# Row maxima of attention scores: one VectorE instruction for two heads, over two neighbouring PSUM banks

## The chip, the core and the metric

One NeuronCore of a Trainium2 chip runs the whole kernel. The metric is the device time of one execution in microseconds (us). The engines are TensorE (PE: matmuls and transposes; PEld: its weight loads), VectorE (DVE), ScalarE (ACT), GpSimd (POOL) and SyncE (SP, which here only issues DMAs). Each engine runs its own instructions in order; they meet only at semaphores.

## What is computed

A gated cross-attention block and a quantised gated feed-forward, each with a residual. B is 8 items of S = 256 rows and E = 256 columns; 16 heads of width 16. Cut to what matters:

```python
def xattn(Q, ctx):                      # Q = layernorm(x)
    q, k, v = heads(Q @ Wq.T), heads(ctx @ Wk.T), heads(ctx @ Wv.T)   # (8, 16, 256, 16)
    attn = where(mask, q @ k.T / sqrt(16), -inf)                      # (8, 16, 256, 256)
    return merge(softmax(attn, axis=-1) @ v) @ Wo.T + bo

x = x + tanh(g_xattn) * xattn(layernorm(x), ctx)
x = x + tanh(g_ffn) * ffn(layernorm(x))     # ffn: 8-bit fake quantisation, silu(gate) * up, down
```

All masks are true in the inputs used, so that the branch without masks runs.

## The kernel before, in words

**Parts of the program.** (1) Projections of the eight items to q, k, v. q and k are split into three bf16 parts, stored to DRAM and loaded back as stacks (`q_st`, `k_st`). The projections of items 6 and 7 are mixed with the first scores of item 0. (2) The attention, one step for each item b. (3) The feed-forward. The change touches the end of (1) and all of (2).

**The softmax in two passes.** The exponentials need the maximum of each score row beforehand. So the scores are computed twice. For the maxima, `scores_for_max` (L1408; `early_scores`, L1314, for item 0) computes 256 x 256 scores of one head with rows on partitions: two matmuls for the two row halves c = 0, 1, side by side in one PSUM bank of 512 f32 columns. `maxima` (L910) takes the negated maximum of both halves with one `tensor_reduce` into `neg_max[:, p, c, h]`. TensorE transposes the maxima of eight heads at a time (`max_tr`, L1298), ScalarE copies them to SBUF (`max_copy`, L724), GpSimd splits them into two bf16 parts (`max_split`, L544 and L545), and a DMA from SyncE's queue puts them as extra rows under `q_st` (`max_rows`, L419). Then `scores_for_exp` (L1422) computes the transposed scores less the maximum, ScalarE takes the exponential (`exp`, L763), and `product_with_v` (L1439) multiplies by v.

**One step** (b, the same order on each engine, written out in the code). On TensorE, for h = 0 to 15: scores for the exponential of head h of item b; then the scores for the maxima of head h+2 of item b+1 (for h = 14 and 15: heads 0 and 1 of item b+2); then what the table `PE_AT` puts at this h: at h = 1 the `max_tr` of heads 8 to 15 of item b and the second half of the product with v of item b-1 (`("pv", 1)`), at h = 3 `project_out` of row half 1 (L1448), at h = 9 the `max_tr` of heads 0 to 7 of item b+1 and `("pv", 0)`, at h = 11 `project_out` of row half 0. On VectorE, for h = 0 to 15: what `DVE_AT` puts at h, then `maxima` of head h of item b+1. `DVE_AT` gives: h = 3 `back` (L1033), h = 4 `turn` (L1009, waits for the product with v), h = 5 the reciprocals (`rec`, L1015), h = 9 `back` (waits for GpSimd's `scale_heads`, L578), h = 12 `row_max` (L1060, from step 3 on), two `stats` (L1047, from step 2 on) and `turn`, h = 13 `rec` and `means` (L1055).

**PSUM banks.** The scores for the maxima go to `bank_b`, four banks, head h in bank h % 4. TensorE may write head h only when the maximum of head h-4 has been taken: `pe.wait_ge(max_done, H * b + h - 3)`, and `maxima` waits for `a_done`, one count for each head. The scores for the exponential rotate over three banks of `bank_a` and wait for ScalarE's `exp`.

**GpSimd in one step:** `max_split` of heads 8 to 15 of item b (it gates the exponential scores of heads 8 and later, over the DMA), `add_bias`, `v_copy`, `residual` (L570), `scale_heads` (L578; gates `back`), `max_split` of heads 0 to 7 of item b+1, `residual` (waits for ScalarE's `scaled_out`, L772), `scale_heads`, and for item b-2 `second_rstd` (L493 to L500) and `hat` (L561).

**The end of the projections.** `project_and_maxima` (L989) on VectorE takes, for each of items 6 and 7, two maxima, a `residue` (L995), two maxima, a `residue`, and four more maxima. TensorE interleaves `early_scores` with the projection's matmuls.

Of the kernel before, what the change touches and what calls it, by code (L numbers as in the profile page):

```python
# [21 lines left out]
P = 128  # L22
ALU = mybir.AluOpType
ACT = mybir.ActivationFunctionType
AX = mybir.AxisListType
# [40 lines left out]
def flamingo_block(nc, x, ctx_in, mask_rows, mask_full, g_xattn, g_ffn, Wq, Wk, Wv, Wo, bo,  # L66
# [3 lines left out]
    H = 16  # L70
    D = E // H
    EC = E // P
    QC = S // P
# [12 lines left out]
    HH = H // 2  # L86
# [40 lines left out]
    with ExitStack() as stack:  # L127
        def sb(name, shape, dt=F32):
            return stack.enter_context(nc.sbuf_tensor(name, shape, dt))

        def pb(name, shape, dt=F32):
            return stack.enter_context(nc.psum_tensor(name, shape, dt))

        def sem(name):
            return stack.enter_context(nc.semaphore(name))
# [14 lines left out]
        ident_f = sb("ident_f", [P, P])  # L150
# [2 lines left out]
        tg_bo = sb("tg_bo", [P, E])  # L153
        wd_scale = sb("wd_scale", [P, E])
        wd_diag = sb("wd_diag", [P, EC, P])
        neg_max = sb("neg_max", [P, 2, QC, H])
        max_f = sb("max_f", [HH, 2, S])
        max_parts = sb("max_parts", [HH, 2, 2, S], BF16)
        rec = sb("rec", [P, 2, NB])
# [70 lines left out]
        bank_b = pb("bank_b", [P, 4, 512])  # L230
# [33 lines left out]
        a_done, max_done = sem("a_done"), sem("max_done")  # L264
# [71 lines left out]
        def at_head(places, h, b, p, known=B, ahead=True):  # L336

            return [(what, b - at // H if at >= H else b, (p, 1 - p)[at // H % 2]) for what, at in places.items()
                    if at % H == h and at // H <= known and (ahead or "next" not in what)]
# [537 lines left out]
        def _(dve):  # L877
# [29 lines left out]
                dve.wait_ge(ct_done, b + 1)  # L907
                dve.tensor_copy(ctx_t[:, p], bank_b[:, 2 + p]).then_inc(ctx_t_ready, 1)

            def maxima(b, p, h, bank):  # L910
                dve.wait_ge(a_done, H * b + h + 1)
                dve.tensor_reduce(neg_max[:, p, :, h], bank.rearrange("p (c s) -> p c s", c=QC),  # L912
                                  axis=AX.X, op=ALU.max, negate=True).then_inc(max_done, 1)

            def residue(b, p, w):
                dve.wait_ge(hi_done, 2 * b + w + 1)
# [72 lines left out]
            def project_and_maxima(b, p, first):  # L989

                for w in range(2):
                    maxima(0, 0, first + 2 * w, bank_b[:, 2 * w])
                    maxima(0, 0, first + 2 * w + 1, bank_b[:, 2 * w + 1])
                    dve.wait_ge(hi_done, 2 * b + w + 1)
                    dve.tensor_tensor(resid[:, p, w], bank_a[:, w], parts[:, p, w, HI[w]], ALU.subtract  # L995
                                      ).then_inc(res_done, 1)
                for h in range(first + 4, first + HH):
                    maxima(0, 0, h, bank_b[:, h % 4])

            project_and_maxima(6, 0, 0)  # L1000
            project_and_maxima(7, 1, HH)


# [90 lines left out]
            def other(what, b, p):  # L1094
                if what[0] == "row_max":
                    row_maxima(b)
                elif what[0] == "means":
                    row_means(b, p)
                elif what[0] == "stats":
                    row_stats(b, what[1])  # L1100
                elif what[0] == "turn":
                    turn(b, what[1])
                elif what[0] == "rec":
                    reciprocals(b, what[1])
                else:
                    back(b, p, what[1])

            def step(b, p, known=B):


                for h in range(H):
                    for what, of, q in at_head(DVE_AT, h, b, p, known):
                        other(what, of, q)
                    maxima(b + 1, 1 - p, h, bank_b[:, h % 4])

            def groups(b, pair, g=slice(0, 2), turns=1):

# [33 lines left out]
            for b in range(B - 1):  # L1151
                step(b, b % 2, b)
# [110 lines left out]
        def _(pe):  # L1263
            mm, tr = nc.tensor.matmul, nc.tensor.transpose
# [28 lines left out]
            def max_tr(b, p, half, to, used):  # L1293
                if used:
                    pe.wait_ge(*used)
                pe.wait_ge(max_done, H * b + HH * (half + 1))
                for c in range(QC):
                    done = tr(to[0:HH, c * P:(c + 1) * P], neg_max[:, p, c, HH * half:HH * (half + 1)], ident_f[:])  # L1298
                done.then_inc(mt_done, 1)

            def early_scores(h, masked):
# [62 lines left out]
            def project_and_scores(b, p, j, first, masked):  # L1364

                def scores(n):
                    early_scores(first + n, masked)
                    if first and n == 1:
                        max_tr(0, 0, 0, bank_m, (w_ready, 4))

                project(b, p, j, ahead=False, between=scores)
                for n in range(6, HH):
                    scores(n)
# [27 lines left out]
            def attend(masked):  # L1401
# [50 lines left out]
                def other(what, b, p, of, q, known):  # L1452

                    if what == "max_tr":
                        max_tr(b, p, 1, ring_bank(b, what), ring_free(b, what, known))
                    elif what == "next_max_tr":
                        max_tr(b + 1, 1 - p, 0, ring_bank(b, what), ring_free(b, what, known))
                    elif what[0] == "out":
                        project_out(of, q, min(what[1], 1), ring_bank(b, what), ring_free(b, what, known))
                    else:  # L1460
                        for g in range(2 * what[1], 2 * what[1] + 2):
                            product_with_v(of, q, g, known == 0 and g == 0)
# [179 lines left out]
```

## Time and profile before

| | us |
|---|---|
| median of 3 executions | 254.37 (254.21 to 257.52) |
| the profiled execution, own time | 256.14 |
| its span, first to last instruction | 254.6 |
| VectorE busy | 212.6 (84%) |
| TensorE busy | 212.0 (83%) |
| ScalarE busy | 160.1 (63%) |
| GpSimd busy | 138.0 (54%) |
| mean granted TensorE clock | 0.960 |

The profile is of one execution. Its own time stands 1.5 us above its span, and it is 1.8 us (0.7%) above the median of the three; the durations below are the profile's. A busy share is an average over stages with different limits, so that it names no bound by itself.

### The profile page before, as it was taken

What the parts mean: (1) busy time and instruction counts of PE and PEld (TensorE: products, weight loads), DVE (VectorE), ACT (ScalarE), POOL (GpSimd) and SP (SyncE); (2) the same over time, 40 slices, a digit from 0 to 9 for tenths busy, and PEclk for the clock granted to TensorE, in tenths of its full rate; (3) what the DMA queues carried; (4) which work ended last, traced back from release to release, by engine and by line L of the source; (5) the groups of instructions that cost most, each with busy time, mean ns of one, the idle gap of its engine ahead of it and who ended that gap; (6) DMA issues with size and microseconds to landing.
All of it is one profiled execution on the core that took longest, in us unless ns stands there. A gap on an engine that the chain in (4) does not pass through costs nothing.

```text
span 254.6 us, 5343 instructions
## 1 busy us (share of the span) xinstructions
PE 212.0 (83%) x1661; PEld 145.1 (57%) x1664; DVE 212.6 (84%) x419; ACT 160.1 (63%) x293; POOL 138.0 (54%) x241
## 2 busy tenths in 40 slices
PE   0899799979989999999999999989592898853970
PEld 0688688857746666666666666645361443312850
DVE  3378699979898998988989898969957779998992
ACT  2347476476687766667677666677726588865920
POOL 7446467643452536285675838389835433330590
PEclk9999999999999999999999999999979599996897
DMA  6999948999546653455436152000000600000296
GB/s 219 236 295 295 299 134 226 272 258 259 145 140 167 130 124 97 102 127 125 128 98 139 45 138 83 4 0 4 1 0 0 206 3 1 0 4 0 25 144 167
DMA packets 34185, 30.80 MB, mean 121 GB/s; under 512 B 5232, under 2 KB 27760, under 8 KB 34160
## 3 DMA queue, kind: packets, MB, share of 16 engines
q1 hardware_dynamic: 29776, 27.74, 40.2%
q0 software_dynamic: 1360, 1.31, 4.2%
q10 hardware_dynamic: 3024, 1.44, 2.1%
q8 instruction: 13, 0.21, 0.4%
q14 instruction: 12, 0.10, 0.1%
HBM read 20.65 MB, written 9.70 MB: 119 GB/s over the span
## 4 chain that ended last, share of the span: by engine, by line
PE 35%; DVE 27%; issue 10%; ACT 9%; POOL 7%; DMA 5%; SPq 4%; ACTq 0%; POOLq 0%; DVEq 0%
PE bank_o L1439 9%; PE bank_a L1422 6%; PE bank_b L1408 4%; PE bank_a L1448 3%; ACT arena L763 3%; DVE h_max L1200 3%; PE bank_a L1325 3%; DMA big<-in_ctx 3%; DVE big L1209 2%; DMA big<-max_parts 2%; DVE arena L1237 2%; DVE arena L902 2%; DVE v_all L1243 2%; POOL big L486 1%; DVE resid L917 1%
## 5 line engine op out<-in xcount | busy, mean ns | idle before, releaser
L912 DVE TENSOR_REDUCE neg_max<-bank_b 128x2 f32<-128x512 f32 x128 | 80.1, 672 | 4.9 <-PE bank_b L1314 3.0
L1422 PE MATMUL bank_a<-big 98*128 98x256 bf16 x256 | 48.8, 274 | 6.2 <-ACT arena L763 2.3
L763 ACT ACTIVATE arena<-bank_a 128x512 f32<-128x512 f32 x64 | 34.3, 605 | 13.9 <-PE bank_a L1422 13.8
L1408 PE MATMUL bank_b<-big 96*128 96x256 bf16 x224 | 42.7, 272 | 0.3 <-issue 0.2
L763 ACT ACTIVATE big<-bank_a 128x512 f32<-128x512 f32 x64 | 33.9, 595 | 12.4 <-PE bank_a L1422 12.1
L1422 PEld LDWEIGHTS bank_a<-big 98*128 98x128 bf16 x256 | 20.2, 97 | 25.4 <-issue 8.8
L1325 PE MATMUL bank_a<-arena,w_t 128*128 128x256 f32 x128 | 30.8, 387 | 0.2 <-issue 0.2
L1325 PEld LDWEIGHTS bank_a<-arena,w_t 128*128 128x128 f32 x128 | 23.6, 194 | 3.6 <-issue 0.6
L510 POOL TENSOR_TENSOR arena<-resid,arena 128x512 bf16<-128x512 f32 x16 | 18.3, 1160 | 10.7 <-ACT arena L701 10.7
L1408 PEld LDWEIGHTS bank_b<-big 96*128 96x128 bf16 x224 | 21.1, 97 | 4.5 <-issue 0.8
L570 POOL TENSOR_TENSOR x_rows<-x_rows,arena 128x256 f32<-128x256 f32 x14 | 11.6, 833 | 15.4 <-ACT arena L772 15.4
L850 ACT ACTIVATE arena<-bank_b,w_scale_x 128x512 f32<-128x512 f32 (+1 forms) x24 | 16.1, 685 | 6.0 <-PE bank_b L1574 2.0
L650 POOL TENSOR_TENSOR big<-arena 128x512 f32<-128x512 f32 x8 | 10.1, 1267 | 17.3 <-ACT arena L854 17.3
L1574 PE MATMUL bank_b<-arena,wgu_t 128*128 128x512 bf16 (+1 forms) x57 | 16.2, 394 | 3.1 <-DVE big L1209 2.9
L544 POOL CAST max_parts<-max_f 8x256 bf16<-8x256 f32 x16 | 6.4, 399 | 21.9 <-issue 19.4
L692 ACT ACTIVATE arena<-bank_a 128x512 bf16<-128x512 f32 x16 | 9.4, 595 | 13.3 <-PE bank_a L1325 8.2
L1009 DVE STREAM_TRANSPOSE arena<-bank_o 128x512 f32<-128x512 f32 (+1 forms) x17 | 11.5, 679 | 7.3 <-PE bank_o L1439 7.3
L1439 PE MATMUL bank_o<-arena,v_cur 128*32 128x256 f32 x256 | 15.7, 382 | 1.3 <-DVE arena L1009 1.3
L1336 PE MATMUL bank_o<-w_t,arena 128*128 128x256 f32 x64 | 15.6, 381 | 0.0
L1439 PE MATMUL bank_o<-big,v_cur 128*32 128x256 f32 x256 | 15.5, 382 | 0.0
L1200 DVE TENSOR_REDUCE h_max<-big 128x1 f32<-128x512 f32 (+1 forms) x24 | 15.1, 668 | 0.0
L1448 PE MATMUL bank_a<-w_t,arena 128*128 128x256 f32 x56 | 14.5, 381 | 0.1
(179 smaller groups left out, 437.7 us busy)
## 6 DMA issues: line engine op xcount, KB each, us to landing
qk_parts<-arena SPq DMA_DIRECT2D x8, 768.0 KB, 5.5
big<-qk_parts SPq DMA_DIRECT2D x32, 192.0 KB, 3.3
big<-qk_parts SPq DMA_DIRECT2D x32, 128.0 KB, 3.3
x_rows<-in_x SPq DMA_DIRECT2D x8, 256.0 KB, 6.3
big<-qk_parts SPq DMA_DIRECT2D x32, 64.0 KB, 3.5
big<-in_ctx SPq DMA_DIRECT2D x7, 256.0 KB, 4.9
out<-x_rows SPq DMA_DIRECT2D x7, 256.0 KB, 2.8
out<-v_all POOLq DMA_DIRECT2D x5, 256.0 KB, 6.3
```

Source lines behind the costliest of these rows:

```text
L510: pool.tensor_tensor(parts[:, p, w, LO[w]], resid[:, p, w], parts[:, p, w, MID[w]], ALU.subtract).then_inc(lo_done, 1)
L763: act.activation(probabilities(h), ring_bank(b, ("exp", h)).rearrange("p (c s) -> p c s", c=QC), ACT.Exp, scale=SCALE).then_inc(exp_done, 1)
L850: act.activation(silu[0:r, c % 3], bank_b[0:r, c % 3], ACT.Silu, scale=w_scale_x[0:r, c:c + 1]).then_inc(silu_done, 1)
L912: dve.tensor_reduce(neg_max[:, p, :, h], bank.rearrange("p (c s) -> p c s", c=QC), axis=AX.X, op=ALU.max, negate=True).then_inc(max_done, 1)
L1200: chain.then(dve.tensor_reduce(h_max[0:r, tile(u)], h_all[0:r, c, bass.ds(n * CW, CW)], axis=AX.X, op=ALU.max, apply_absolute_value=True))
L1325: last = mm(bank_a[:, w, f * S:(f + 1) * S], w_t[:, w, k, f * P:(f + 1) * P], src[:, p, k * S:(k + 1) * S], start=(k == 0), stop=(k == EC ...
L1336: last = mm(bank_o[:, c * E:(c + 1) * E], ctx_t[:, p, k * S + c * P:k * S + (c + 1) * P], w_t[:, 2, k], start=(k == 0), stop=(k == EC - 1))
L1408: done = mm(to, q_st[0:KR, p, h, c * P:(c + 1) * P], k_st[0:KR, p, h], start=True, stop=not masked)
L1422: done = mm(to, k_st[0:KM, p, h, k * P:(k + 1) * P], q_st[0:KM, p, h], start=True, stop=not masked)
L1439: done = mm(bank_o[n * 2 * D:(n + 1) * 2 * D, g % 2 * S:(g % 2 + 1) * S], v_cur[:, p, k, h], probabilities(h)[:, k], start=(k == 0), stop= ...
L1448: done = mm(to[:, 0:E], att_t[:, p, f, c * P:(c + 1) * P], w_t[:, 3, f], start=(f == 0), stop=(f == EC - 1))
L1574: last = mm(to, wgu_t[:, g, k, c * P:c * P + r], xq_t[:, k, bass.ds(n * CW, CW)], start=(k == 0), stop=(k == EC - 1))
```

## The change

`neg_max` is laid out with the row halves innermost. `maxima` now takes heads h and h+1 (h even) in one `tensor_reduce` that reads banks h % 4 and h % 4 + 1 (four rows of 256 columns for each partition) and writes four neighbouring values; it waits until the scores of both heads are there and raises `max_done` by 2 at its end. In the steps it is issued at odd h, behind what `DVE_AT` puts there; at even h only the items of the table are issued. TensorE's order and all its waits stay as they are. The transposes of the maxima read `neg_max` with a stride of 2 in place of 1.

```diff
-        neg_max = sb("neg_max", [P, 2, QC, H])
+        neg_max = sb("neg_max", [P, 2, H, QC])
...
-            def maxima(b, p, h, bank):
-                dve.wait_ge(a_done, H * b + h + 1)
-                dve.tensor_reduce(neg_max[:, p, :, h], bank.rearrange("p (c s) -> p c s", c=QC),
-                                  axis=AX.X, op=ALU.max, negate=True).then_inc(max_done, 1)
+            def maxima(b, p, h):
+                banks = bank_b[:, h % 4:h % 4 + 2]
+                dve.wait_ge(a_done, H * b + h + 2)
+                dve.tensor_reduce(neg_max[:, p, h:h + 2], banks.rearrange("p h (c s) -> p h c s", c=QC),
+                                  axis=AX.X, op=ALU.max, negate=True).then_inc(max_done, 2)
...
             def project_and_maxima(b, p, first):
                 for w in range(2):
-                    maxima(0, 0, first + 2 * w, bank_b[:, 2 * w])
-                    maxima(0, 0, first + 2 * w + 1, bank_b[:, 2 * w + 1])
+                    maxima(0, 0, first + 2 * w)
...
-                for h in range(first + 4, first + HH):
-                    maxima(0, 0, h, bank_b[:, h % 4])
+                for h in range(first + 4, first + HH, 2):
+                    maxima(0, 0, h)
...
                     for what, of, q in at_head(DVE_AT, h, b, p, known):
                         other(what, of, q)
-                    maxima(b + 1, 1 - p, h, bank_b[:, h % 4])
+                    if h % 2:
+                        maxima(b + 1, 1 - p, h - 1)
...
-                    done = tr(to[0:HH, c * P:(c + 1) * P], neg_max[:, p, c, HH * half:HH * (half + 1)], ident_f[:])
+                    done = tr(to[0:HH, c * P:(c + 1) * P], neg_max[:, p, HH * half:HH * (half + 1), c], ident_f[:])
```

## Rows read from the trace of the kernel before

**Rows 1.** Part 1 of the page: busy us, share of the span, instructions.
```profile
PE 212.0 (83%) x1661; PEld 145.1 (57%) x1664; DVE 212.6 (84%) x419; ACT 160.1 (63%) x293; POOL 138.0 (54%) x241
```

**Rows 2.** Part 4 of the page: the chain that ended last, by engine, by line.
```profile
PE bank_o L1439 9%; PE bank_a L1422 6%; PE bank_b L1408 4%; PE bank_a L1448 3%; ACT arena L763 3%; DVE h_max L1200 3%; PE bank_a L1325 3%; DMA big<-in_ctx 3%; DVE big L1209 2%; DMA big<-max_parts 2%; DVE arena L1237 2%; DVE arena L902 2%; DVE v_all L1243 2%; POOL big L486 1%; DVE resid L917 1%
```

**Rows 3.** The instructions of line L912, and who waited for them (us, times).
```profile
L912 DVE TENSOR_REDUCE neg_max<-bank_b x128: 627/680/694, 56.0 to 166.5; 128x2 f32<-128x512 f32 x128
...
  PEld bank_b L1408: 0.7, 3
```

**Rows 4.** Two other VectorE reductions, by line and form: count, busy us, mean ns.
```profile
L935 DVE TENSOR_REDUCE mask_sum<-mask_u 128x4 f32<-128x1024 uint8 x4 | 4.8, 1207 | 0.0
...
L983 DVE TENSOR_REDUCE w_amax<-wd_rows 128x2 f32<-128x1408 f32 x1 | 1.6, 1605 | 0.0
```

**Rows 5.** Timeline of VectorE, steps 3 and 7: start us, us, instruction, count.
```profile
117.14 0.45 DVE L1033 STREAM_TRANSPOSE arena<-arena 128x256 f32<-128x256 f32 x1 [0.48 <-POOL arena L578]
117.51 1.85 DVE L912 TENSOR_REDUCE neg_max<-bank_b 128x2 f32<-128x512 f32 x3
119.28 0.67 DVE L1060 TENSOR_REDUCE row_max<-v_all 128x2 f32<-128x512 f32 x1
119.87 0.74 DVE L1047 BATCH_NORM_STATS2 stats<-x_rows 128x6 f32<-128x256 f32 x2
120.53 0.70 DVE L1009 STREAM_TRANSPOSE arena<-bank_o 128x512 f32<-128x512 f32 x1
121.15 0.66 DVE L912 TENSOR_REDUCE neg_max<-bank_b 128x2 f32<-128x512 f32 x1
...
121.98 3.65 DVE L912 TENSOR_REDUCE neg_max<-bank_b 128x2 f32<-128x512 f32 x6
...
180.08 0.70 DVE L1009 STREAM_TRANSPOSE arena<-bank_o 128x512 f32<-128x512 f32 x1
180.81 0.25 DVE L1017 RECIPROCAL rec<-arena 128x16 f32<-128x16 f32 x1
```

**Rows 6.** Timeline of TensorE, from head 8 of step 3 to head 8 of step 4.
```profile
116.62 0.39 PE L1422 MATMUL bank_a<-big 98*128 98x256 bf16 x2 [0.16 <-DMA big<-max_parts]
...
122.32 0.38 PE L1422 MATMUL bank_a<-big 98*128 98x256 bf16 x2
122.54 0.38 PE L1408 MATMUL bank_b<-big 96*128 96x256 bf16 x2
...
123.63 0.39 PE L1422 MATMUL bank_a<-big 98*128 98x256 bf16 x2 [0.27 <-ACT arena L763]
...
124.88 1.93 PE L1439 MATMUL bank_o<-arena,v_cur 128*32 128x256 f32 x32
...
131.06 0.39 PE L1422 MATMUL bank_a<-big 98*128 98x256 bf16 x2 [0.24 <-DMA big<-max_parts]
```

**Rows 7.** Timeline of VectorE where step 0 begins.
```profile
68.62 9.06 DVE L912 TENSOR_REDUCE neg_max<-bank_b 128x2 f32<-128x512 f32 x15 [0.29 <-PE bank_b L1314]
```

**Rows 8.** Timeline of TensorE where step 0 begins, to the first transpose of maxima.
```profile
69.21 0.60 PE L1408 MATMUL bank_b<-big 96*128 96x256 bf16 x4 [0.19 <-issue]
...
69.97 0.39 PE L1408 MATMUL bank_b<-big 96*128 96x256 bf16 x2
70.20 0.38 PE L1422 MATMUL bank_a<-big 98*128 98x256 bf16 x2
...
70.80 0.38 PE L1298 MATMUL bank_a<-ident_f,neg_max 128*8 128x128 f32 x2
```

**Rows 9.** The chain in order of time at the same place: start us, us, what.
```profile
70.40 1.06 ACT big L763 x2
71.46 0.25 ACT max_f L724
...
73.81 1.77 DMA big<-max_parts
75.63 0.39 PE bank_a L1422 x2
```

## The prediction

> **What bounds the kernel now.** I read the busy times first. VectorE and TensorE are both at five sixths of the span [rows 1], and L912, the line that changes, is the costliest of all: 128 instructions of about 0.68 us [rows 3]. A reader who stops there expects most of what is saved at L912 to be gained.
>
> The chain of waits says otherwise. Among its largest parts are the matmuls L1439, L1422 and L1408, ScalarE's exponential and the DMA of the maxima; of the feed-forward's VectorE work some stands there too; L912 does not [rows 2]. The question from the other side, who waited for L912, gives 0.7 us in all, in three waits [rows 3]. That is all that a shorter L912 alone could give back on TensorE's side. So VectorE is almost full in the attention and yet bounds it hardly anywhere.
>
> One step shows why. It is 14.44 us long (head 8 of step 3 at 116.62, of step 4 at 131.06) [rows 6]. VectorE's cost of an instruction is the distance between starts, since consecutive records overlap: 15 maxima in 9.06 us, each record 0.68 long, make (9.06 - 0.68) / 14 = 0.60 us each [rows 3, 7]. In the same way row_max costs 0.59, the two stats 0.66, a turn 0.62, back 0.37, rec and means together 0.23 (121.98 less the end of the maximum at 121.15 + 0.60) [rows 5]. A step is 16 x 0.60 for the maxima and 0.59 + 0.66 + 2 x 0.62 + 2 x 0.37 + 0.23 + 0.15 (the second rec, an estimate from the first) = 3.6 for the rest, 13.2 us of 14.44. VectorE has 1.2 us to spare in each step and spends part of it waiting for GpSimd before back [rows 5]. Head 8 of each step waits for the DMA that brings the maxima, by 0.24 us in step 4 [rows 6]; that DMA is GpSimd's, and GpSimd's work before it hangs on the previous step's project_out, not on VectorE.
>
> **The change, part by part.**
>
> *The instruction.* No row shows an f32 reduction over two PSUM banks. The nearest are reductions of one row set of 1024 columns, 1.207 us, and of 1408, 1.605 us, 1.04 ns for each further column [rows 4]. Against 0.68 us for 512 columns the second 512 cost 0.53, so that a pair should show a record of about 1.21 us and cost 0.60 + 0.53 = 1.13 us, where two cost 1.20. Saved: 0.07 for each of 64 pairs, 4.3 us of VectorE's time, 0.5 us in a step. Bounds: below, nothing but the columns is paid, 2 x 0.53 = 1.06; above, the two records end to end, 2 x 0.68 = 1.36. I take 1.13, because the 1024-column row is the nearest. By rows 2 and 3 the saving lies beside other work; I book it at 0, at most -0.7 (all that TensorE waited for L912).
>
> The trace thus shows 0.07 us as what an instruction costs beside its columns. The Trainium skill (VectorE: DVE Perf Modes, Side-by-side: where the cycles go for N=2048 bf16) gives some 150 cycles of init and decode for each instruction, and its Rules for kernel authors say to minimise the count of operations. By that, 64 removed instructions would be about 10 us less VectorE work, an estimate from the page; rows 7 say 4.3 at most, because the start of an instruction overlaps the end of the one before.
>
> *The release of banks.* This is the loss. TensorE may write head h when the maximum of head h-4 is taken. Before, an even head was free 0.68 us after its own start; now it is free with the odd one, after 1.21 us, and the instruction cannot start before the odd head's scores are there. Four banks become two pairs.
>
> *Start of step 0.* TensorE's first score matmuls of item 1 run right behind VectorE: the ones at 69.97 come 0.07 after the end of the second record of the run at 68.62 (68.62 + 0.60 + 0.68 = 69.90) [rows 7, 8]. After the change: heads 12 and 13 of item 0 from 68.62 (the run still waits for head 13's scores) to 69.83, heads 14 and 15 from 69.75 to 70.96. Head 0 of item 1 needs head 12: 69.90 instead of 69.21. Head 2 needs head 14, so the second pair: 71.03 instead of 69.97. The exponential scores of head 1 stand behind it in TensorE's queue: 71.25 instead of 70.20; then head 3 and the transpose of the maxima, at 71.7 instead of 70.80. ScalarE copies the maxima behind the exponential of head 1, that is at 72.2 instead of 71.46, and from there the chain runs through GpSimd and the DMA to head 8 at 75.63 [rows 9]. So +0.7 us, on the chain of waits, and what follows (products with v, exponentials) moves with it. Bounds: 0.4 (the second pair ends only 0.45 later than the third of three single maxima, if the order behind it lets the rest be caught up) and 1.0.
>
> In the interleaved part before, each residue (L995) comes about 0.5 later, since its pair ends later than the second single maximum did. ScalarE reads it behind other copies, and only from 69.0 on is it busy without a gap; I book 0, at most +0.2.
>
> *A step with all the extra work (from step 3 on).* Back at 117.14 waits for GpSimd [rows 5]; before, the maximum of head 8 was taken during that wait, now heads 8 and 9 come behind back. From its end at 117.51: two pairs 2.26, row_max 0.59, stats 0.66, turn and rec 0.62 + 0.23, and a wait of rec for turn. That wait was hidden by a maximum between them; rows 5 show it bare in step 7, 180.08 to 180.81, 0.73 against 0.62, so 0.1. Heads 12 and 13 start at 121.97, are done at 123.18. TensorE wants bank 0 for head 0 of the item after next at 122.54, at h = 14 [rows 6]: it stalls until 123.25, 0.7 us. Behind it wait the exponential scores of head 15, then ScalarE. Heads 14 and 15 are done 1.13 later, at 124.31; head 2 is written at 124.38, the exponential scores of head 1 at 124.60, the transpose 125.04, and the product with v at 125.35 instead of 124.88: +0.47. Until head 8, ScalarE's four exponentials are late by that, and head 8 waits for the DMA anyway (0.24) and for the exponential of head 5; there some 0.2 to 0.3 is left. That delay reaches GpSimd through project_out and comes back to back one step later, so that it counts once in two steps. Steps 3, 4 and 5 have the stall (step 6 issues no scores ahead at h = 14): 0.1 each, +0.3. Bounds: 0 (all hidden by the DMA wait) and 3 x 0.47 = +1.4.
>
> Rec now runs right behind turn, ahead of the next maxima, so GpSimd's scale_heads and second_rstd are not made late by it. The waits that the change adds hold no other engine's DMA. The strided read in the transposes concerns 32 weight loads of 8 columns; 0.
>
> *Sum.* 0 + 0.7 + 0 + 0.3 = +1.0 us. For the profiled execution 256.14 + 1.0 = 257.1, span 255.6. The profiled execution stood 0.7% above the median, so for the median 254.37 + 1.0 = 255.4.
>
> **The rivals.**
>
> *A: VectorE's time counts.* If the chain is only apparent, and every step is in truth paced by VectorE's 13.2 us with its waits, all of 4.3 us comes back: 250.1. For it: 84% busy. Against it: 0.7 us of waits for L912, and a wait for TensorE or GpSimd in each step. It decides where a step's idle time on VectorE is gone; a partial form gives 252.
>
> *B: two banks in one read cost more than 1.13.* At 1.36 a step is 8 x 1.36 + 3.7 = 14.6 us, above 14.44: VectorE becomes the bound, 0.15 in each of 6 steps, and the stalls above grow by 3 x 0.23 = 0.7 each, of which steps 3 to 5 pass on most. With 0.7 + 0.3 at the start that is 0.9 + 1.0 + 2.1 = 4.0, so 258.4. The point from which it decides is (14.44 - 3.7) / 8 = 1.34 us for a pair.
>
> *C: the stall at h = 14 is passed on whole.* Where the TensorE-ScalarE loop itself is the bound, nothing hides it: +0.7 at the start and 1.4 to 2.1 in steps 3 to 5, 256.5 to 257.2, taken as 256.8.
>
> *D: nothing is seen.* The start is caught up during step 0, where VectorE is ahead, and the rest is hidden: 254.4.
>
> The Trainium skill (Advanced Engine Details and Errata, TRN2 Errata) lists reading several PSUM banks with one instruction among its workarounds; that speaks against B, and no row here shows such a read.
>
> **How the numbers follow.** The forecast (+0.5 to +1.5) has 0.40, C 0.18, D 0.20, A 0.10 (a third of it below 251), B 0.12. The predicted time is 255.4. The range goes down to the partial form of A, 252.3, and up beyond B's 258.4 to 258.6. 2% is 5.1 us, about what a measurement of this kernel can tell from no change: faster than 249.3 needs more than all of A, 0.03; slower than 259.5 needs a pair beyond 1.36 us, half of B, 0.06; within, 0.91.
>
> **What would show each step right or wrong.** L912 should be 64 records of 1.2 us with 128x4 outputs; VectorE's busy time lower by some 3 us, TensorE's the same, its idle time up. In step 0 head 8 should start near 76.3. L1408 should wait for L912 well beyond 0.7 us, mostly once a step at h = 14 from step 3 on. Rec should follow turn at once. The forecast is wrong if the span falls by over 2 us (then A), if a pair's record is 1.3 us or more (B), or if head 8 of step 0 stays at 75.6 (D).

## The result and the profile after

The changed kernel takes 1.0086 times the time before, 95% interval 1.0054 to 1.0118, over 20 executions of each. Both figures leave out the executions that took over 1.5% longer than the fastest of their kernel, 5 before and 3 after. On the median that the prediction started from, 254.37 us, that is 256.6 us: +2.2 us where +1.0 was forecast, outside the forecast's own band of +0.5 to +1.5 and within 2%. The profiled execution shows 257.1 us of span against 254.6.

The instruction is what was expected, and it did not help. Line L912 is now L913 (lines behind it move by one or stay). Part 5 of the page and, below it, who waited for L913 (us, times), the rows that answer to [rows 3] and [rows 4]:

```profile
L913 DVE TENSOR_REDUCE neg_max<-bank_b 128x4 f32<-128x1024 f32 x64 | 75.5, 1210 | 9.6 <-PE bank_b L1315 4.9
```

```profile
  PE bank_b L1315: 4.9, 6
  PE bank_b L1409: 4.2, 8
...
  PEld bank_b L1409: 3.5, 8
  PE bank_b L1409: 2.5, 6
  PE bank_b L1315: 0.2, 1
```

The first two lines of the second fence are VectorE waiting for scores before L913; the last three are TensorE and its weight loads waiting for L913. Those were 0.7 us in three waits before [rows 3]; they are 3.5 us in 8 waits and 2.5 us in 6 now (the two overlap: the matmul at 125.25 below waits 0.59 us and its weight load 0.87, for the same record of L913), and 0.2 us in one wait of the early scores, L1315. And L913 has entered the chain that ended last, where L912 was absent [rows 2]; part 4 of the page, by line:

```profile
PE bank_o L1440 8%; PE bank_a L1423 6%; PE bank_b L1409 6%; DVE neg_max L913 4%; DMA big<-in_ctx 3%; DVE h_max L1201 3%; PE bank_a L1449 3%; PE bank_a L1326 2%; DVE big L1210 2%; DVE arena L1238 2%; DVE arena L902 2%; DVE v_all L1244 2%; DVE stats L1047 1%; DVE arena L1009 1%; ACT arena L763 1%
```

**Where the time went.** Two executions drift apart by a few tenths of a microsecond before the changed part begins (the first early score matmul starts at 55.60 before, 55.91 after). Measured from that matmul, the attention repeats within 0.01 us from run to run where its waits are the same, as layout_only below shows, so I use the stretch that begins there as a ruler. Its end is the product with v at h = 1 of step 7, the last in the chain ahead of the closing VectorE work, which starts at 168.26 before and 170.83 after: 112.66 and 114.92 us from the ruler's start, +2.26. (The product with v behind it, at h = 9 of step 7, is 2.11 later than before.) From there to the end of the span both take 86.3 us, so that in these two executions the whole loss lies in the changed part. Three stretches of each, up to the ruler, the ruler, and behind it (from:to, us; busy us and instructions of PE, PEld, DVE, ACT and POOL; granted TensorE clock, DMA share, GB/s):

```profile
0.00:55.60 55.60, 45.11 (x231) 38.69 (x232) 41.10 (x96) 28.60 (x52) 32.53 (x75) 1.00 0.88 248
55.60:168.26 112.66, 106.64 (x1024) 71.79 (x1028) 102.08 (x196) 79.44 (x164) 62.18 (x112) 1.00 0.47 120
168.26:254.60 86.34, 60.23 (x410) 34.58 (x413) 69.47 (x128) 52.09 (x79) 43.28 (x56) 0.88 0.20 41
```

```profile
0.00:55.91 55.91, 46.22 (x231) 39.64 (x232) 40.73 (x96) 28.84 (x52) 32.81 (x75) 1.00 0.89 248
55.91:170.83 114.92, 107.41 (x1025) 71.42 (x1027) 100.31 (x132) 80.00 (x164) 62.04 (x112) 1.00 0.45 117
170.83:257.10 86.27, 60.94 (x414) 34.62 (x413) 69.57 (x128) 52.10 (x80) 42.91 (x56) 0.86 0.20 41
```

The granted clock is 1.00 (2.4 GHz) over the ruler in all ten profiles, so that it has no part in what the ruler shows. Behind the ruler it is 0.86 to 0.89 and the stretch takes 83.7 to 86.3 us, with the same code in every run: that the two kernels agree there to 0.1 us is chance, and spans of single executions can't show an effect of 2 us.

Timelines of TensorE in the changed kernel, the places where the time goes:

```profile
55.91 0.38 PE L1315 MATMUL bank_b<-big 96*128 96x256 bf16 x2
...
63.20 0.38 PE L1315 MATMUL bank_b<-big 96*128 96x256 bf16 x2 [0.18 <-DVE neg_max L913]
...
70.71 0.60 PE L1409 MATMUL bank_b<-big 96*128 96x256 bf16 x4 [1.04 <-DVE neg_max L913]
...
71.76 0.39 PE L1409 MATMUL bank_b<-big 96*128 96x256 bf16 x2 [0.23 <-DVE neg_max L913]
71.98 0.38 PE L1423 MATMUL bank_a<-big 98*128 98x256 bf16 x2
...
72.43 0.38 PE L1299 MATMUL bank_a<-ident_f,neg_max 128*8 128x128 f32 x2
...
77.18 0.39 PE L1423 MATMUL bank_a<-big 98*128 98x256 bf16 x2 [1.08 <-DMA big<-max_parts]
```

From the ruler's start, head 0 of item 1 comes at 14.80 (before 13.61, [rows 8]), the transpose of the maxima at 16.52 (before 15.20), head 8 of step 0 at 21.27 (before 20.03): +1.24. Before that stands a stall that the prediction had not seen, at 63.20: head 8 of item 0 waits for the pair of heads 4 and 5. The same matmul started at 62.55 before, 6.95 from the start; now 7.29, +0.34. VectorE's row that answers to [rows 7]:

```profile
69.34 8.08 DVE L913 TENSOR_REDUCE neg_max<-bank_b 128x4 f32<-128x1024 f32 x7 [0.35 <-PE bank_b L1315]
```

It begins 13.43 us from the ruler's start, 0.41 later than before (68.62 - 55.60 = 13.02). Its first pair, heads 12 and 13, ends at 69.34 + 1.22 = 70.56, and head 0 of item 1 follows at 70.71 in the fence above. The chain that ended last goes through the second pair, heads 14 and 15, into head 2 of item 1 at 71.76 and on to ScalarE, the rows that answer to [rows 9]:

```profile
70.48 1.23 DVE neg_max L913
...
71.76 0.39 PE bank_b L1409 x2
72.15 0.23 PE bank_a L1423 x2
...
72.41 0.60 ACT big L763
73.00 0.26 ACT max_f L724
```

In step 3, TensorE and VectorE of the changed kernel:

```profile
124.28 0.38 PE L1423 MATMUL bank_a<-big 98*128 98x256 bf16 x2
125.25 0.39 PE L1409 MATMUL bank_b<-big 96*128 96x256 bf16 x2 [0.59 <-DVE neg_max L913]
```

```profile
119.10 0.45 DVE L1033 STREAM_TRANSPOSE arena<-arena 128x256 f32<-128x256 f32 x1 [0.63 <-POOL arena L578]
119.47 2.32 DVE L913 TENSOR_REDUCE neg_max<-bank_b 128x4 f32<-128x1024 f32 x2
121.70 0.67 DVE L1060 TENSOR_REDUCE row_max<-v_all 128x2 f32<-128x512 f32 x1
122.29 0.74 DVE L1047 BATCH_NORM_STATS2 stats<-x_rows 128x6 f32<-128x256 f32 x2
122.95 0.70 DVE L1009 STREAM_TRANSPOSE arena<-bank_o 128x512 f32<-128x512 f32 x1
123.68 0.25 DVE L1015 RECIPROCAL rec<-arena 128x16 f32<-128x16 f32 x1
123.85 0.23 DVE L1055 BATCH_NORM_AGGREGATE mv_now<-stats 128x2 f32<-128x6 f32 x2
124.00 3.45 DVE L913 TENSOR_REDUCE neg_max<-bank_b 128x4 f32<-128x1024 f32 x3
```

The reader is to compare the two fences: head 0 of the item after next stands behind 124.28 in TensorE's queue and wants its bank at 124.50; the pair of heads 12 and 13 starts at 124.00 and ends at 125.21; the matmul starts at 125.25. Between back (119.10, which waited for GpSimd) and that pair now stand the maxima of four heads, row_max, stats, turn, rec and means; between back and the maximum of head 12 there stood three maxima, row_max, stats and turn before [rows 5].

### The profile page after: what moved, and what is told of

The parts are those of the page before. It is cut to its first block, busy times and chain, and to the rows that moved or that the text cites. A ratio compares the mean times of both kernels' runs of the same rounds, so it can differ in the third digit from the quotient of the medians.

```text
span 257.1 us, 5346 instructions
## 1 busy us (share of the span) xinstructions
PE 214.6 (83%) x1664; PEld 145.7 (57%) x1664; DVE 210.6 (82%) x355; ACT 160.9 (63%) x293; POOL 137.8 (54%) x241
## 4 chain that ended last, share of the span: by engine, by line
PE 35%; DVE 33%; issue 11%; ACT 7%; POOL 5%; DMA 4%; SPq 3%; ACTq 0%; DVEq 0%; POOLq 0%
PE bank_o L1440 8%; PE bank_a L1423 6%; PE bank_b L1409 6%; DVE neg_max L913 4%; DMA big<-in_ctx 3%; DVE h_max L1201 3%; PE bank_a L1449 3%; PE bank_a L1326 2%; DVE big L1210 2%; DVE arena L1238 2%; DVE arena L902 2%; DVE v_all L1244 2%; DVE stats L1047 1%; DVE arena L1009 1%; ACT arena L763 1%
## 5 line engine op out<-in xcount | busy, mean ns | idle before, releaser
L913 DVE TENSOR_REDUCE neg_max<-bank_b 128x4 f32<-128x1024 f32 x64 | 75.5, 1210 | 9.6 <-PE bank_b L1315 4.9
L1326 PE MATMUL bank_a<-arena,w_t 128*128 128x256 f32 x128 | 32.1, 399 | 0.5 <-issue 0.5
L1326 PEld LDWEIGHTS bank_a<-arena,w_t 128*128 128x128 f32 x128 | 24.5, 201 | 4.3 <-issue 0.9
L1409 PEld LDWEIGHTS bank_b<-big 96*128 96x128 bf16 x224 | 20.3, 97 | 9.3 <-DVE neg_max L913 3.5
L1575 PE MATMUL bank_b<-arena,wgu_t 128*128 128x512 bf16 (+1 forms) x60 | 17.1, 398 | 2.6 <-DVE big L1210 2.6
```

The costliest lines, as they stand in the source:

```text
L913: dve.tensor_reduce(neg_max[:, p, h:h + 2], banks.rearrange("p h (c s) -> p h c s", c=QC), axis=AX.X, op=ALU.max, negate=True).then_inc(ma ...
L1326: last = mm(bank_a[:, w, f * S:(f + 1) * S], w_t[:, w, k, f * P:(f + 1) * P], src[:, p, k * S:(k + 1) * S], start=(k == 0), stop=(k == EC ...
L1409: done = mm(to, q_st[0:KR, p, h, c * P:(c + 1) * P], k_st[0:KR, p, h], start=True, stop=not masked)
L1575: last = mm(to, wgu_t[:, g, k, c * P:c * P + r], xq_t[:, k, bass.ds(n * CW, CW)], start=(k == 0), stop=(k == EC - 1))
```

## Experiments

The ruler of each run (same two marks in its own chain and timeline), beside the ratio to the kernel before:

| run | ruler, us | against before | ratio (95% interval) |
|---|---|---|---|
| before | 112.66 | | |
| after | 114.92 | +2.26 | 1.0086 (1.0054 to 1.0118) |
| layout_only | 112.66 | 0.00 | 0.9967 (0.9926 to 1.0008) |
| pairs_start_only | 113.89 | +1.23 | 1.0042 (1.0005 to 1.0080) |
| pairs_steps_only | 113.69 | +1.03 | 1.0025 (0.9988 to 1.0062) |
| pairs_back_later | 114.49 | +1.83 | 1.0063 (1.0023 to 1.0103) |
| pairs_steps_back_later | 113.18 | +0.52 | 1.0007 (0.9968 to 1.0046) |
| pairs_but_last_four | 112.94 | +0.28 | 0.9988 (0.9951 to 1.0026) |
| single_half_columns | 112.66 | 0.00 | 1.0000 (0.9963 to 1.0037) |
| pairs_half_columns | 112.74 | +0.08 | 0.9992 (0.9944 to 1.0039) |

The intervals of the ratios are some 0.4% to each side, 1 us, so that most of these runs can't be told from each other by their times. The ruler resolves them, from one profiled execution each. The times confirm it where they can: the intervals of after, pairs_start_only and pairs_back_later lie above 1, and those of the others include it.

**layout_only**

`maximum` is the reduction of one head in the new layout; it stands in project_and_maxima too.

```diff
+            def maximum(b, p, h):
+                dve.wait_ge(a_done, H * b + h + 1)
+                dve.tensor_reduce(neg_max[:, p, h], bank_b[:, h % 4].rearrange("p (c s) -> p c s", c=QC),
+                                  axis=AX.X, op=ALU.max, negate=True).then_inc(max_done, 1)
...
-                    if h % 2:
-                        maxima(b + 1, 1 - p, h - 1)
+                    maximum(b + 1, 1 - p, h)
```

> The changed layout of neg_max and the transposes that read it with a stride of 2, but one instruction for each head as before, so this leaves only the layout of the change. Theory (the loss comes from the later release of banks): no difference, ratio 1.000 within 0.002, L912's instructions at 0.68 us, the waits for them under 1 us as before. Rival (the strided weight loads or the denser writes cost): part of the 1.0086, that is 1.003 to 1.009, with transposes of the maxima above 0.27 us.

Measured: ruler +0.00, ratio 0.9967. The layout, the denser writes and the strided transposes cost nothing. The transposes of the maxima have the same 272 ns and the wait for L912 the same 0.7 us as before.

**pairs_start_only and pairs_steps_only**

pairs_start_only has the last three lines of the edit above, on the changed kernel. pairs_steps_only leaves the steps of the changed kernel and has:

```diff
-                    maxima(0, 0, first + 2 * w)
+                    maximum(0, 0, first + 2 * w)
+                    maximum(0, 0, first + 2 * w + 1)
...
-                for h in range(first + 4, first + HH, 2):
-                    maxima(0, 0, h)
+                for h in range(first + 4, first + HH):
+                    maximum(0, 0, h)
```

> Pairs in the maxima of item 0 (project_and_maxima) alone, single maxima in all steps. Theory: TensorE waits for the pairs of heads 4, 5 and 12 to 15 of item 0; head 8 of step 0 starts 1.0 us later against the start of the projections of item 6, and nothing makes this good later: +1.1 us, ratio 1.004. Rival (the start is caught up in step 0, all loss is in the steps): ratio 1.000.

> Single maxima for item 0, pairs in all steps. Theory: step 0 begins as before; 0.4 us are lost in steps 0 and 1 at heads 0, 8 and 10 of the next item, and 0.6 us in steps 3 to 5 at h = 14 (a wait of 0.6 us for L912 in step 3): +1.0 us, ratio 1.004. Rival (the steps give back the saved VectorE time once the start does not hide it): ratio below 1.000, down to 0.985 if all 0.5 us of each step counts.

Measured: +1.23 and +1.03, together 2.26, exactly what the whole change costs. Eight of the 64 pairs make over half of the loss. In pairs_start_only the head 8 of step 0 is 1.23 late and stays 1.23 late in every product with v to the end: nothing is caught up, and nothing is added. In pairs_steps_only step 0's head 8 comes at 20.03 from the ruler's start, as before; the product with v at h = 1 of step 2 comes at 41.24, where it came at 40.83, so 0.41 late; the other 0.62 come in steps 3 to 5. So the rival, that the steps give back VectorE's saved time, is out.

**pairs_back_later and pairs_steps_back_later**

```diff
-              ("rec", 1): H + 5, ("back", 1): H + 9,
+              ("rec", 1): H + 5, ("back", 1): H + 10,
```

> The changed kernel with back of the second pair of groups moved from h = 9 to h = 10 in VectorE's order, so that the maxima of heads 8 and 9 are taken while GpSimd's scale_heads is awaited, as the maximum of head 8 was before. Theory: heads 12 and 13 are done 0.6 to 1.1 us earlier in steps 3 to 5, the wait of TensorE at h = 14 falls from 0.6 us to under 0.1, and 0.6 us come back: +1.6 us against the kernel before, ratio 1.006. Rival (the steps are held by the TensorE-ScalarE loop or GpSimd alone and the stall is hidden): ratio unchanged at 1.0086.

> Single maxima for item 0, pairs in the steps, back moved from h = 9 to h = 10. Theory: the losses add, so of 1.0 us for the pairs in the steps the 0.4 us are given back that the move gave back beside pairs at the start: last product with v 0.6 us later than before against the first scores of item 0, ratio 1.0024. Rival (the two are not independent): 1.0 us, or 0.

Measured: +1.83 and +0.52, so that the move of one instruction in VectorE's order gives back 0.43 and 0.51 of the 0.62 us of steps 3 to 5. VectorE of pairs_back_later at the same place:

```profile
117.37 2.50 DVE L913 TENSOR_REDUCE neg_max<-bank_b 128x4 f32<-128x1024 f32 x2 [0.52 <-PE bank_b L1409]
119.79 0.43 DVE L1033 STREAM_TRANSPOSE arena<-arena 128x256 f32<-128x256 f32 x1
120.14 1.19 DVE L913 TENSOR_REDUCE neg_max<-bank_b 128x4 f32<-128x1024 f32 x1
121.25 0.67 DVE L1060 TENSOR_REDUCE row_max<-v_all 128x2 f32<-128x512 f32 x1
```

Two pairs now stand ahead of back, which no longer waits for GpSimd, and row_max starts at 121.25 where it started at 121.70. TensorE's matmuls in this run have no wait for L913 left in step 3, and the weight load ahead of the second one 0.27 us (0.87 in the changed kernel):

```profile
124.42 0.38 PE L1423 MATMUL bank_a<-big 98*128 98x256 bf16 x2
124.80 0.39 PE L1409 MATMUL bank_b<-big 96*128 96x256 bf16 x2
```

The matmul comes 0.38 behind its neighbour instead of 0.97, so the wait in the records is gone, though not the last 0.16 us over the usual 0.22. Of the 0.19 and 0.11 us that are left of the 0.62, 0.12 and 0.11 come in one place: at h = 14 of step 5 the matmul still waits for L913, by 0.21 us, and the product with v behind it is that much later.

**pairs_but_last_four** (on pairs_steps_only)

```diff
+                    if h >= 12:
+                        maximum(b + 1, 1 - p, h)
-                    if h % 2:
+                    elif h % 2:
                         maxima(b + 1, 1 - p, h - 1)
```

> Single maxima for item 0; in the steps pairs for heads 0 to 11 and single maxima for heads 12 to 15, in the order of the kernel before; back at h = 9. 42 pairs are left of 64, so 2.8 us of VectorE time are saved as against 4.3. Theory: head 12 is done before TensorE wants its bank at h = 14, so the 0.6 us in steps 3 to 5 and 0.15 us in step 0 go; 0.25 us stay, for the pairs of heads 4 to 7 in step 1; ratio 1.001. Rival (every pair costs a little, wherever it is): two thirds of the 1.0 us of the steps, ratio 1.003.

Measured: +0.28. 42 pairs cost 0.28 us, of which 0.24 come in step 1, as expected; the 14 of heads 12 to 15 cost 0.75. What pairs cost depends on where they stand, and not on their number.

**single_half_columns and pairs_half_columns**

The first edit is on the kernel before, the second on the changed one.

```diff
-                  bank.rearrange("p (c s) -> p c s", c=QC),
+                  bank.rearrange("p (c s) -> p c s", c=QC)[:, :, 0:S // 2],
```

```diff
-                  banks.rearrange("p h (c s) -> p h c s", c=QC),
+                  banks.rearrange("p h (c s) -> p h c s", c=QC)[:, :, :, 0:S // 2],
```

> The kernel before, but each maximum is taken over the first 128 of the 256 columns of a row half; the other columns are left out, all else is the same work. L912 should fall from 0.68 to 0.41 us, 34 us of VectorE time in all. Theory (VectorE's time in the attention does not bound): the whole kernel gains 0 to 1.5 us, ratio 0.994 to 1.000. Rival (the 84% busy VectorE paces the steps): over 10 us faster, ratio under 0.96.

> The changed kernel, but each maximum is taken over the first 128 of the 256 columns of a row half; the other columns are left out. A pair's record should then be 0.68 us, as long as that of one head before. Theory (what costs is how long a pair holds two banks, not that two heads are tied together): TensorE no longer waits for L912 beyond what it did before, the loss of 2.2 us is gone, time within 0.5 us of the single maxima over half the columns, ratio 0.994 to 1.002. Rival (waiting for the odd head's scores is itself the cost): still over 1 us slower than the single maxima over half the columns.

Measured: 0.00 and +0.08. The record of one head fell to 0.411 us, as expected, and VectorE's busy time by 28 us, not by 34, since consecutive records overlap. The page and the instructions of L912 in single_half_columns:

```profile
PE 211.8 (83%) x1661; PEld 145.6 (57%) x1664; DVE 184.4 (73%) x419; ACT 160.1 (63%) x293; POOL 138.1 (54%) x241
```

```profile
L912 DVE TENSOR_REDUCE neg_max<-bank_b x128: 360/425/427, 56.4 to 166.5; 128x2 f32<-128x256 f32 x128
its engine sat idle before it (us, times) until:
  PE bank_b L1408: 13.2, 20
  PE bank_b L1314: 6.0, 9
```

VectorE is busy 28 us less than in [rows 1], and the ruler does not move by 0.01 us: the time is now idle time before L912 (19.2 us against 4.6), before turn (13.8 against 4.8) and before back (5.1 against 1.9). That is the clearest answer to rival A. It also shows that the 0.7 us of waits for L912 [rows 3] were worth nothing: they are 0.2 us here. In pairs_half_columns the instructions and the waits for them:

```profile
L913 DVE TENSOR_REDUCE neg_max<-bank_b x64: 652/692/693, 57.2 to 166.2; 128x4 f32<-128x512 f32 x64
...
who waited for it (us, times):
  PE bank_b L1409: 0.5, 1
```

A pair that holds its two banks for 0.69 us instead of 1.21 costs 0.08 instead of 2.26 us, although it still waits for the odd head's scores and takes the same place in VectorE's order. So the coupling of two heads by itself is worth 0.08 us at this length; the rest is the time for which the pairs hold their banks and stand in front of each other in VectorE's queue. The run shortens both together and does not part them.

## Why the prediction came out as it did

- **The bound.** Right. VectorE at 84% of the span bounded nothing in the attention: taking away 28 us of its work changed nothing there. Its busy time fell by 2.0 us with the change, 212.6 to 210.6, where some 3 was forecast. Rival A is refuted. The two rows that said so beforehand were the absence of L912 in the chain and the 0.7 us of waits for it.
- **The instruction.** Right. The record was forecast at 1.21 us and is 1.210; the distance between starts was forecast at 1.13 and is (8.08 - 1.22) / 6 = 1.14 in a run of seven from 69.34 and 1.12 in the run of three above. Rival B is refuted: a read over two neighbouring PSUM banks costs what its columns cost, 1.210 us beside the 1.207 us of 1024 columns in [rows 4]. The Trainium skill (Advanced Engine Details and Errata, TRN2 Errata) lists reading several PSUM banks with one instruction among its workarounds, and the trace agrees that it can be done.
- **The start of step 0.** The mechanism was right, the term was mis-sized: +0.7 forecast, with bounds of 0.4 and 1.0, and +1.23 measured by pairs_start_only. The working from head 12 of item 0 on holds once it starts later. What failed is the sentence on the interleaved part: it looked for who reads the residues and booked 0, and did not follow TensorE's own wait for the banks there. Head 8 of item 0 waits for the pair of heads 4 and 5, 0.34 us, and everything behind it moves; the run of pairs begins 0.41 later, and with the forecast's 0.7 that is 1.1 of the 1.23. The last 0.1 was lost in the forecast's own working: it has the exponential scores of head 1 at 71.25; the exponential follows 0.43 later and the copy of the maxima 0.59 behind that (71.98, 72.41 and 73.00 in the rows above), so the copy belonged at 72.27, +0.8, and not at 72.2, +0.7.
- **Steps 0 to 2.** Missed. The prediction costed only steps with the work of h = 12; 0.41 us are lost in steps 0 and 1, where the scores of heads 0, 2, 8 and 10 of the item ahead come 0.1 to 0.3 us later than usual, behind their pairs. VectorE had more to spare there, but a pair of banks comes back later all the same.
- **Steps 3 to 5.** The mechanism was right, and so were the place and about the size of the stall: 0.7 us forecast at h = 14 of step 3, 0.59 in the record of the wait. The product with v behind it was forecast 0.47 late and is 0.60 later than the ones ahead of it; at h = 9 of step 4 0.30 of that is left, where 0.2 to 0.3 was forecast. What was low is the share that is passed on: I took 0.1 a step from the argument that the delay counts once in two steps, and the steps cost 0.30, 0.16 and 0.16, in all 0.62 instead of 0.3.
- **The sum.** +1.0 forecast, about +2.2 measured: 0.5 too little at the start, 0.4 missed in steps 0 and 1, 0.3 too little in steps 3 to 5. These are the three terms by which the forecast time, 255.4, fell short of 256.6. The change went the way that was forecast, for the reason that was given; less than half of its size was foreseen.
- **Rivals C and D.** C (the stall passed on whole) put 1.4 to 2.1 us into steps 3 to 5; 0.62 was passed on, so its time of 256.8 was close by luck. D (nothing is seen) is excluded by the interval and by the ruler.

What no run settles is why steps 4 and 5 cost 0.16 each and not 0.1; TensorE's records show a wait for L913 of 0.23 and 0.24 us at h = 14 there. No correct version tried beats the kernel before by more than its interval.

## What to carry to other kernels

In this kernel an engine that was busy 84% of the span, and absent from the chain of waits, had no time to give back: ask who waited for the line before making it shorter. Where an instruction also gives back a buffer, fusing two of them halves the number of buffers that the producer sees: count the time from the start of the first to the end of the fused one, with all that stands ahead of it in its queue, against the moment at which the producer wants the first buffer again. And where a fused instruction falls behind a wait that one of its halves used to fill, move the waiting instruction behind it.

## What the runs showed of the hardware

- One VectorE reduction over two neighbouring PSUM banks, 128x1024 f32 to four values, took 1.210 us, beside 0.672 us for one bank: 1.05 ns for each added column, beside 1.04 in the reductions of [rows 4], so nothing for the second bank.
- Weight loads of 128x8 f32 maxima read with a stride of 2 took 88 ns in the mean in layout_only, against 86 ns with a stride of 1 before; the median is 87 ns in both.
- The times of a stretch of 112 us, with five engines and a DMA queue in it, repeated to 0.01 us between executions of two kernels with the same waits, while the whole executions of the kernel before spread over 253.6 to 261.0 us. Effects that are smaller than the 1 us of the intervals could be read and added up in it: 1.23 and 1.03 made 2.26.
